# The head of the expert part of a GNN and mixture-of-experts kernel: one copy of h moved, a register load split, and other filler products on TensorE

## The chip, the cores and the metric

The kernel runs on one core of one Trainium2 chip. The metric is the device time of one execution in microseconds (us). The times of the kernel before are from three timed runs. One more execution was taken with a hardware profiler. The rows below come from that one.

## What is computed

`x` has 625 rows of 256 numbers. A graph part with 20000 edges runs first and gives x1. A feed-forward part with 8 experts follows. It sends every row to the two experts with the highest gate scores:

```python
x = x + gnn(layernorm(x), edge_index, W0, b0, W1, b1, W2, b2, Wf, bf)
xn = layernorm(x)
gate_scores = xn @ Wg + bg                          # 625 x 8
_, idx = top_k(gate_scores, 2)
mask = one_hot(idx, 8).sum(axis=-2)
h = gelu(einsum('td,edh->teh', xn, W1) + b1)        # 256 -> 512
y = einsum('teh,ehd->ted', h, W2) + b2              # 512 -> 256
out = x + einsum('ted,te->td', y, mask)
```

## The kernel before, in words

**Graph part (lines 880 to 1568).** The 20000 edges are turned into one-hot matrices on VectorE (DVE). TensorE (PE) multiplies them into a 625 x 625 count matrix. Three levels of products with that matrix follow, with each float split in a high and a low half. This part is not touched by the change.

**Routing (from L1164).** DVE adds the graph part to x, takes mean and variance, and centres the rows (`xc`). PE transposes `xc` (L1577), ScalarE (ACT) copies it out (L834), and PE makes the gate scores with 20 narrow products (L1585). DVE picks the two best experts of each row and writes the picks as 0 and 1 into `both_bf` (L1199 to L1213). PE sums them with a triangle and with ones (L1592 to L1599, the prefix sums). From these DVE works out the slot of each row: rows are sorted by expert into tiles of 128 slots, and a tile belongs to one expert. DVE then writes one-hot matrices: `hot_slot` for the first two tiles (L1262), `hot_place` and `row_in_tile` for the table of rows (L1282, L1288). The expert number of each tile stands in `owner_i` (L1253).

**The filler products.** While PE would wait in this stretch it multiplies the identity by itself into a bank that nobody reads. This is `keep_busy(n)` (L1335 to L1338). Each of its products is 128x128 float32 by 128 columns, and the profile lists it as two MATMUL records. The counts stand in L78: 12 behind the last graph product, 4 ahead of the scores, `WARM_ROUTE` = 10 between the scores and the wait for `both_bf` (L1589), and `WARM_GATHER` = 24 between the prefix sums and the wait for `hot_slot` (L1643). They are ordinary instructions of PE's queue. What stands behind them waits until they are through.

**Expert part.** `gather` (L1604) makes x of tiles 0 and 1 by products with `hot_slot`, and ACT copies it into `xt` (L862). Ten products (L1650) give `row_of`, the row behind each slot. With it GpSimd (POOL) fetches the x of later tiles by indirect DMA (L617) and adds the results into the output (L623), one scatter at a time. There are 10 fixed tiles (`FIXED`) and then a loop over pairs of tiles. In this run there are 13. A tile s goes through these steps:

- `up(s)`, PE L1620: two products of 512 columns, into `bank[1]` (tile even) or `g_ps[0]` (odd)
- `add_b1(s)`, DVE L1269: adds the expert's b1 and writes `h_pre`
- `gelu(s)`, ACT L855: `h_pre` to `h_act`
- `transpose_h(s)`, PE L1633: four transposes of `h_act` into `bank[2]`
- `h_transposed(s)`, ACT L859: copies `bank[2]` to `h_t`
- `down(s)`, PE L1639: four products into `bank[3]`
- `add_b2(s)`, DVE L1273: adds b2 and writes `y_sb`, from which POOL scatters

x of tiles from 2 on is transposed by PE (`transpose_x`, L1627) and copied by ACT (`x_transposed`, L850).

The order on each engine is written out by hand. On PE the head is up(0), up(1), transpose_h(0), down(0), transpose_x(2), transpose_h(1), up(2), transpose_x(3), down(1). On ACT it is (L863 to L869):

```python
            gelu(0, 0)
            gelu(1, 1)
            for s in range(FIXED):
                h_transposed(s)
                x_transposed(s + 2, s % 2)
                if s:
                    gelu(s + 1, (s + 1) % 2)
```

PE and DVE address the weights and biases of a tile by its expert number, which must be in a register of the engine. `first_experts` (L399 to L404) loads the numbers of the first 11 tiles with one load. PE does it at L1654, DVE at L1300, ahead of `add_b1(0)`. The load shows in the trace as TENSOR_LOAD of the engine's queue.

Of the kernel before, what the change touches and what calls it, by code (L numbers as in the profile page):

```python
# [10 lines left out]
EXPERTS = 8  # L11
# [3 lines left out]
P = 128  # L15
# [59 lines left out]

WARM_DEGREE, WARM_NORM, WARM_GATE, WARM_ROUTE, WARM_GATHER = 10, 12, 4, 10, 24  # L78


MAX_TILES = (2 * NODES + EXPERTS * (P - 1)) // P
# [3 lines left out]
FIXED = -(-2 * NODES // P)  # L85
# [4 lines left out]
def build(nc, x, src, dst, W, B, Wf, bf, Wg, bg, W1, b1, W2, b2, out):  # L90
# [8 lines left out]
    with ctx:  # L99
        def sb(name, shape, dt, scope=ctx):  # L100
            return scope.enter_context(nc.sbuf_tensor(name, shape, dt))
# [11 lines left out]
        ident = sb("ident", [P, P], f32)  # L113
        ones_sq = sb("ones_sq", [P, P], f32r)
        ones_bf = sb("ones_bf", [P, P], bf16)
# [107 lines left out]
        owner_i = sb("owner_i", [1, SLOT_TILES + 1], i32, ffn)  # L223
# [16 lines left out]
        bank = [ctx.enter_context(nc.psum_tensor(f"bank{i}", [P, 512], f32)) for i in range(2)]  # L240
# [149 lines left out]
        def gather_ps():  # L390
            return bank[0].rearrange("p (k s) -> p k s", k=KC)
# [4 lines left out]
        def odd_tile(eng):  # L396
            return eng.value_load(pairs_i[0:1, 1:2], min_val=0, max_val=1)

        def first_experts(kind):  # L399

            _, ids = nc.values_load_multi_w_load_instructions(
                owner_i[0:1, 0:FIXED + 1], engines=(kind,), min_val=0, max_val=EXPERTS - 1,
                skip_runtime_bounds_check_because="a count of at most EXPERTS, cut to EXPERTS - 1 just above")
            return ids  # L404

        def up_bank(s):
            return (bank[1], g_ps[0])[s % 2]
# [265 lines left out]
        def _(act):  # L673
# [22 lines left out]
            def chunk_starts(a):  # L696

                _, starts = nc.values_load_multi_w_load_instructions(
                    base_i[0:1, a:a + 8], engines=(mybir.EngineType.Activation,), min_val=0, max_val=NODES - 1,
                    skip_runtime_bounds_check_because="the least of a chunk's node numbers, which are below NODES")  # L700
                return starts
# [146 lines left out]
            def x_transposed(s, h):  # L848
                act.wait_ge(x_t_done, s - 1)
                act.copy(xt[:, :, h * P:(h + 1) * P], bank[0][:, 0:D].rearrange("p (k s) -> p k s", k=KC))\  # L850
                    .then_inc(xt_ready, 1)

            def gelu(s, h):
                act.wait_ge(pre_ready, s + 1)
                act.activation(h_act[:, h, :], h_pre[:, h, :], ACT.Gelu).then_inc(act_ready, 1)  # L855

            def h_transposed(s):
                act.wait_ge(t_done, s + 1)
                act.copy(h_t[:], bank[2].rearrange("p (k s) -> p k s", k=HC)).then_inc(h_t_ready, 1)  # L859

            act.wait_ge(gathered, 1)
            act.copy(xt[:], gather_ps()).then_inc(xt_ready, 2)  # L862
            gelu(0, 0)  # L863
            gelu(1, 1)
            for s in range(FIXED):
                h_transposed(s)
                x_transposed(s + 2, s % 2)
                if s:
                    gelu(s + 1, (s + 1) % 2)  # L869
            act.wait_ge(experts_ready, 2)  # L870
            more = pairs(act)
            with act.Fori(0, more) as p:
                for h in range(2):
                    s = p * 2 + (FIXED + h)
# [8 lines left out]
        def _(dve):  # L883
            n = [0]
# [382 lines left out]
            def add_b1(s, h, e):  # L1267
                dve.wait_ge(up_done, s + 1)
                dve.tensor_tensor(h_pre[:, h, :], up_bank(h)[:, :], b1_bc[:, ds(e, 1), :], ALU.add).then_inc(pre_ready, 1)  # L1269

            def add_b2(s, b, e):
                dve.wait_ge(down_done, s + 1)
                dve.tensor_tensor(y_sb[:, b, :], bank[3][:, 0:D], b2_bc[:, ds(e, 1), :], ALU.add).then_inc(y_ready, 1)  # L1273
# [23 lines left out]
            dve.scalar_tensor_tensor(row_of[:], rows_1, -1.0, unused[:], ALU.add, ALU.add).then_inc(rows_ready, 1)  # L1297
            dve.wait_ge(experts_ready, 2)
            dve.wait_ge(ffn_b_in, 16 * (EXPERTS + 1))
            e_of = first_experts(mybir.EngineType.DVE)  # L1300
            add_b1(0, 0, e_of[0])
            add_b1(1, 1, e_of[1])
            for s in range(FIXED):
                if s:
                    dve.wait_ge(act_ready, s)
                    add_b1(s + 1, (s + 1) % 2, e_of[s + 1])
                if s >= 4:
                    dve.wait_ge(scattered, 16 * (s - 3))
                add_b2(s, s % 4, e_of[s])
            more = pairs(dve)  # L1310
            with dve.Fori(0, more) as p:
                for h in range(2):
                    s = p * 2 + (FIXED + h)
# [6 lines left out]
            with dve.If(odd_tile(dve) > 0):  # L1320
                s = more * 2 + FIXED
# [5 lines left out]
        def _(pe):  # L1327
# [4 lines left out]
                pe.matmul(out_, lh, rl, start=False, stop=False, skip_group_check=True)  # L1332
                return pe.matmul(out_, ll, rh, start=False, stop=last, skip_group_check=True)  # L1333

            def keep_busy(n, free=3):  # L1335

                for _ in range(n):
                    pe.matmul(bank[free][:, 0:P], ident[:], ident[:], start=True, stop=True)  # L1338


            pe.wait_ge(consts, 4)
# [59 lines left out]
            for i, (h, c) in enumerate(Z_OUT):  # L1401
                a, b = HALVES[h]
# [166 lines left out]


            keep_busy(WARM_NORM)
            for t in range(NT):
                pe.wait_ge(xc_ready, t + 1)
                if t >= 2:
                    pe.wait_ge(xc_t_ready, t - 1)
                for k in range(KC):
                    last = pe.transpose(bank[t % 2][:, k * P:(k + 1) * P], xc[:, t, k * P:(k + 1) * P], ident[:])  # L1577
                last.then_inc(xc_t_ps, 1)
            keep_busy(WARM_GATE)
            pe.wait_ge(ffn_w_in, 16 * (2 + 2 * EXPERTS))  # L1580
            for t in range(NT):
# [4 lines left out]
                                     skip_group_check=True)  # L1586
            last.then_inc(score_ps, 1)

            keep_busy(WARM_ROUTE)  # L1589
            pe.wait_ge(both_ready, 1)  # L1590
            total, before = bank[4][:, 128:128 + EXPERTS], bank[4][:, 256:256 + NT * EXPERTS]
            pe.matmul(before, tri_bf[:], both_bf[:].rearrange("p t e -> p (t e)"), start=True, stop=False,  # L1592
                      skip_group_check=True)
            for j in range(1, NT):

                pe.matmul(before[:, j * EXPERTS:], ones_bf[:], both_bf[:, 0:NT - j, :].rearrange("p t e -> p (t e)"),
                          start=False, stop=j == NT - 1, skip_group_check=True)
# [19 lines left out]
            def up(s, h, e):  # L1617
                pe.wait_ge(xt_ready, s + 1)
                for k in range(KC):
                    last = pe.matmul(up_bank(h)[:, :], xt[:, k, h * P:(h + 1) * P], w1_sb[:, ds(e, 1), k, :],  # L1620
                                     start=k == 0, stop=k == KC - 1)
                last.then_inc(up_done, 1)
# [25 lines left out]
            for k in range(2):  # L1648
                for t in range(NT):
                    last = pe.matmul(bank[4][:, 0:SLOT_TILES], hot_place[:, k, t, :], row_in_tile[:, k, :, t],  # L1650
                                     start=k == 0 and t == 0, stop=k == 1 and t == NT - 1)
            last.then_inc(row_ps, 1)
            pe.wait_ge(experts_ready, 2)
            e_of = first_experts(mybir.EngineType.PE)  # L1654
            up(0, 0, e_of[0])
            up(1, 1, e_of[1])
            for s in range(FIXED):
# [9 lines left out]
            with pe.Fori(0, more) as p:  # L1667
                for h in range(2):
                    s = p * 2 + (FIXED + h)
# [7 lines left out]
            with pe.If(odd_tile(pe) > 0):  # L1677
                s = more * 2 + FIXED
# [27 lines left out]
```

## Time and profile before

| what | value |
|---|---|
| three timed runs, median (lowest to highest) | 203.26 us (201.93 to 204.81) |
| the profiled execution, its own time | 204.21 us |
| its span from first to last instruction | 202.4 us |
| mean granted TensorE clock in it | 0.913 of full speed |
| PE busy | 164.4 us (81%) |
| DVE busy | 100.7 us (50%) |
| ACT busy | 70.3 us (35%) |
| POOL busy | 69.8 us (34%) |

Engines work side by side, so busy times add up to more than the span. The profile names an instruction by its line in the code, and its time is counted from the start of the span. In the chain of work that ended last, PE pieces are given without overlap, each from the point where the one before it ends. In the timeline the same instructions have their full durations, which overlap.

### The profile page before, as it was taken

To read this page: it belongs to the slowest core of one execution; us is meant where nothing else is said; L and a number is where in the kernel's file an instruction comes from. 1 tells how busy PE (TensorE), PEld (TensorE's weight loads), DVE (VectorE), ACT (ScalarE), POOL (GpSimd) and SP (SyncE) were. 2 spreads that over 40 slices of the span, in tenths; PEclk is the share of its full clock that TensorE was granted. 3 is DMA by queue.
4 is the path that set the end of the run, shared out by engine and by line. 5 is a ranking of instruction groups with operands and counts; after the bars stand their busy time and mean duration, and the time that the engine had idled before them with its cause. 6 is when DMAs were issued, how large, how long until landed. Compare 5 with 4: busy or idle time off the path is not lost.

```text
span 202.4 us, 3153 instructions
## 1 busy us (share of the span) xinstructions
PE 164.4 (81%) x1013; PEld 135.6 (67%) x1014; DVE 100.7 (50%) x259; ACT 70.3 (35%) x199; POOL 69.8 (34%) x96
## 2 busy tenths in 40 slices
PE   0443575877999999999999889996999999999700
PEld 0332354766899788989899879983676677657500
DVE  7799988784660447224534876922232232223100
ACT  7234984551400136112421076013334343433200
POOL 8506910003029075002000200005555666564560
PEclk9999995585579999999999996999999999999975
DMA  5469999500000501000000179902143235432332
GB/s 144 158 165 378 367 366 368 193 0 5 3 3 0 159 5 47 7 3 3 0 3 0 48 199 279 375 32 78 11 69 80 52 52 71 77 63 26 53 52 26
DMA packets 15784, 20.34 MB, mean 100 GB/s; under 512 B 1482, under 2 KB 12116, under 8 KB 15636
## 3 DMA queue, kind: packets, MB, share of 16 engines
q1 hardware_dynamic: 12420, 15.75, 24.2%
q0 software_dynamic: 2544, 3.54, 10.5%
q10 hardware_dynamic: 800, 0.79, 1.1%
q8 instruction: 12, 0.20, 0.4%
q14 instruction: 8, 0.07, 0.1%
HBM read 16.81 MB, written 3.26 MB: 99 GB/s over the span
## 4 chain that ended last, share of the span: by engine, by line
PE 66%; DVE 13%; DMA 7%; issue 4%; ACT 4%; POOL 2%; ACTq 1%; POOLq 0%; DVEq 0%
PE cnt_ps L1639 9%; PE bank L1620 5%; PE bank L1487 5%; PE cnt_ps L1338 5%; PE g_ps L1620 4%; DMA out_rows<-y_sb,row_put 4%; PE cnt_ps L1487 4%; PE bank L1331 3%; PE g_ps L1331 3%; PE g_ps L1332 3%; PE g_ps L1333 3%; DVE hot_lo L950 2%; PE bank L1333 2%; PE bank L1332 2%; DVE a_hi L1030 2%
## 5 line engine op out<-in xcount | busy, mean ns | idle before, releaser
L1639 PE MATMUL cnt_ps<-w_sb,h_t 128*128 x104 | 24.8, 381 | 2.7 <-ACT h_t L859 2.7
L1639 PEld LDWEIGHTS cnt_ps<-w_sb,h_t 128*128 128x128 f32 x104 | 18.7, 190 | 5.2 <-issue 3.2
L623 POOL DMA_INDIRECT out_rows<-y_sb,row_of x10 | 15.9, 1586 | 15.5 <-DMA out_rows<-y_sb,row_of 11.6
L617 POOL DMA_INDIRECT xg<-x_rows,row_of x12 | 12.0, 1003 | 23.4 <-DVE row_of L1297 20.1
L1379 PE MATMUL bank<-hot_key,hot_lo 125*128 125x45 bf16 (+4 forms) x80 | 8.3, 244 | 12.8 <-DVE hot_key L953 7.9
L1379 PEld LDWEIGHTS bank<-hot_key,hot_lo 125*128 125x128 bf16 x80 | 5.3, 124 | 15.4 <-DVE hot_key L953 13.2
L1273 DVE TENSOR_TENSOR y_sb<-cnt_ps,b_bc 128x256 f32<-128x256 f32 x13 | 5.5, 425 | 20.0 <-PE cnt_ps L1639 20.0
L950 DVE TENSOR_TENSOR hot_lo<-iota_lo,edge_rel 125x1024 bf16<-125x1024 int16 x20 | 14.2, 710 | 0.9 <-PE g_ps L1379 0.7
L1338 PE MATMUL cnt_ps<-ident 128*128 128x128 f32 x100 | 13.5, 297 | 0.0
L1620 PE MATMUL bank<-w_sb,xt 128*128 x28 | 13.4, 599 | 0.1
L1338 PEld LDWEIGHTS cnt_ps<-ident 128*128 128x128 f32 x100 | 12.9, 211 | 0.0
L1620 PE MATMUL g_ps<-w_sb,xt 128*128 x24 | 11.3, 593 | 0.0
L1269 DVE TENSOR_TENSOR h_pre<-bank,b_bc 128x512 f32<-128x512 f32 x7 | 4.8, 692 | 12.5 <-PE bank L1620 12.5
L859 ACT COPY h_t<-cnt_ps 128x512 f32<-128x512 f32 x13 | 7.6, 584 | 9.6 <-PE cnt_ps L1633 9.6
L855 ACT ACTIVATE h_act<-h_pre 128x512 f32<-128x512 f32 x13 | 8.2, 629 | 7.6 <-DVE h_pre L1269 7.6
L850 ACT COPY xt<-bank 128x256 f32<-128x256 f32 x12 | 4.5, 373 | 17.6 <-PE bank L1627 17.6
L1379 PE MATMUL g_ps<-hot_key,hot_lo 125*128 125x45 bf16 (+4 forms) x80 | 8.4, 245 | 2.4 <-ACT a_hi L708 1.5
L1487 PE MATMUL bank<-a_hi,ys_hi 128*128 128x384 f32 x30 | 10.1, 337 | 0.0
L1487 PE MATMUL bank<-a_hi,ys_lo 128*128 128x384 f32 x30 | 10.1, 337 | 0.0
L953 DVE TENSOR_TENSOR hot_key<-key_tables,edge_rel 125x360 bf16<-125x360 int16 (+4 forms) x20 | 9.7, 486 | 0.0
L1331 PE MATMUL g_ps<-w_hi,ht_hi 128*128 128x256 f32 x30 | 9.6, 319 | 0.0
L1332 PE MATMUL g_ps<-w_lo,ht_hi 128*128 128x256 f32 x30 | 9.4, 313 | 0.0
(279 smaller groups left out, 433.9 us busy)
## 6 DMA issues: line engine op xcount, KB each, us to landing
w_sb<-in_L_ffn_W SPq DMA_DIRECT2D x16, 512.0 KB, 10.2
b_bc<-in_L_ffn_b SPq DMA_DIRECT2D x8, 256.0 KB, 5.3
w_stage<-in_L_gnn_W SPq DMA_DIRECT2D x3, 512.0 KB, 5.6
w_stage<-in_L_gnn_Wf SPq DMA_DIRECT2D x4, 256.0 KB, 6.4
b_bc<-in_L_ffn_b SPq DMA_DIRECT2D x1, 1024.0 KB, 12.3
x_rows<-x_f ACTq DMA_DIRECT2D x1, 640.0 KB, 8.7
x_sb<-in_x SPq DMA_DIRECT2D x1, 512.0 KB
out_rows<-x_sb SPq DMA_DIRECT2D x1, 512.0 KB
```

What stands on the lines that cost most here:

```text
L617: pool.indirect_dma_start(out=xg[:, b, :], out_offset=None, in_=x2_rows, in_offset=bass.IndirectOffsetOnAxis(ap=rows, axis=0)).then_inc(x_ ...
L623: pool.indirect_dma_start(out=out, out_offset=bass.IndirectOffsetOnAxis(ap=rows, axis=0), in_=y_sb[:, b, :], in_offset=None, compute_op=AL ...
L950: dve.tensor_tensor(hot_lo[:, u % RING:u % RING + 2, :, :], iota_lo[0:EP].unsqueeze(1).broadcast_to((EP, 2, P, CT)), rel[:, 0].unsqueeze(2 ...
L953: dve.tensor_tensor(hot_keys(u, 2), turn_keys(u // UNROLL)[0:EP].rearrange("p n w i -> p (n w) i").unsqueeze(1) .broadcast_to((EP, 2, NT * ...
L1331: pe.matmul(out_, lh, rh, start=first, stop=False, skip_group_check=True)
L1332: pe.matmul(out_, lh, rl, start=False, stop=False, skip_group_check=True)
L1333: return pe.matmul(out_, ll, rh, start=False, stop=last, skip_group_check=True)
L1338: pe.matmul(bank[free][:, 0:P], ident[:], ident[:], start=True, stop=True)
L1379: last = pe.matmul(pane(k), hot_lo[:, u % RING, :, i], hot_keys(u)[:, 0, :, i], start=i == i0, stop=i == i0 + n_i - 1, skip_group_check=True)
L1487: step = pe.matmul(z_bank(i), y[:, u, m], a_t[:, u, cols], start=first and u == 0 and y is y_parts[0], stop=last and u == NT - 1 and y is ...
L1620: last = pe.matmul(up_bank(h)[:, :], xt[:, k, h * P:(h + 1) * P], w1_sb[:, ds(e, 1), k, :], start=k == 0, stop=k == KC - 1)
L1639: last = pe.matmul(bank[3][:, 0:D], h_t[:, k, :], w2_sb[:, ds(e, 1), k, :], start=k == 0, stop=k == HC - 1)
```

## The change

Three edits, all between the gate scores and the end of tile 0.

1. ACT copies h of tile 0 (`h_transposed(0)`) between gelu(0) and gelu(1), where it stood behind gelu(1). The rest of ACT's order is as before: x_transposed(2), then for s from 1 on h_transposed(s), x_transposed(s + 2), gelu(s + 1).
2. DVE loads the expert numbers of tiles 0 and 1 first, issues add_b1(0) and add_b1(1), and then loads the other nine. PE loads its 11 with one load as before.
3. The 10 float32 filler products in the wait for `both_bf` become 36 products of `ones_bf` by `ones_bf` in bfloat16, 128x128 by 128 columns, into the same unread bank (`keep_clock`). The other three groups of fillers stay as they are.

```diff
-WARM_DEGREE, WARM_NORM, WARM_GATE, WARM_ROUTE, WARM_GATHER = 10, 12, 4, 10, 24
+WARM_DEGREE, WARM_NORM, WARM_GATE, WARM_ROUTE, WARM_GATHER = 10, 12, 4, 36, 24
...
-        def first_experts(kind):
+        def experts_of(kind, a, b):
 
             _, ids = nc.values_load_multi_w_load_instructions(
-                owner_i[0:1, 0:FIXED + 1], engines=(kind,), min_val=0, max_val=EXPERTS - 1,
+                owner_i[0:1, a:b], engines=(kind,), min_val=0, max_val=EXPERTS - 1,
...
             gelu(0, 0)
+            h_transposed(0)
             gelu(1, 1)
-            for s in range(FIXED):
+            x_transposed(2, 0)
+            for s in range(1, FIXED):
                 h_transposed(s)
                 x_transposed(s + 2, s % 2)
-                if s:
-                    gelu(s + 1, (s + 1) % 2)
+                gelu(s + 1, (s + 1) % 2)
...
-            e_of = first_experts(mybir.EngineType.DVE)
+            e_of = experts_of(mybir.EngineType.DVE, 0, 2)
             add_b1(0, 0, e_of[0])
             add_b1(1, 1, e_of[1])
+            e_of = e_of + experts_of(mybir.EngineType.DVE, 2, FIXED + 1)
...
-            def keep_busy(n, free=3):
+            def keep_busy(n):
 
                 for _ in range(n):
-                    pe.matmul(bank[free][:, 0:P], ident[:], ident[:], start=True, stop=True)
+                    pe.matmul(bank[3][:, 0:P], ident[:], ident[:], start=True, stop=True)
+
+            def keep_clock(n):
+
+                for _ in range(n):
+                    pe.matmul(bank[3][:, 0:P], ones_bf[:], ones_bf[:], start=True, stop=True)
...
-            keep_busy(WARM_ROUTE)
+            keep_clock(WARM_ROUTE)
...
-            e_of = first_experts(mybir.EngineType.PE)
+            e_of = experts_of(mybir.EngineType.PE, 0, FIXED + 1)
```

## Rows read from the trace of the kernel before

**Rows 1.** The page, chain that ended last by engine, and one costliest group (busy, mean ns | idle before)

```profile
PE 66%; DVE 13%; DMA 7%; issue 4%; ACT 4%; POOL 2%; ACTq 1%; POOLq 0%; DVEq 0%
...
L1639 PE MATMUL cnt_ps<-w_sb,h_t 128*128 x104 | 24.8, 381 | 2.7 <-ACT h_t L859 2.7
```

**Rows 2.** The chain that ended last, from the scores on: start us, us, what

```profile
121.88 3.59 PE cnt_ps L1338 x20
...
125.58 0.13 PE bank L1599 x5
125.72 5.72 PE cnt_ps L1338 x48
```

**Rows 3.** Timeline of DVE in the routing: start us, us, engine, line, operation [idle before]

```profile
124.26 0.20 DVE L1213 TENSOR_TENSOR both_bf<-both,valid 128x40 bf16<-128x40 f32 x1
125.75 0.17 DVE L1219 TENSOR_SCALAR tiles_i<-bank 128x8 int32<-128x8 f32 x1 [1.29 <-PE bank L1599]
...
129.19 1.56 DVE L1262 TENSOR_TENSOR hot_slot<-iota_p,hot_pos 128x640 fp32r<-128x640 f32 x2
```

**Rows 4.** Stretches of half a us: stretch, its length, PE busy (instructions), granted clock, DMA

```profile
122.00:122.50 0.50, 0.50 (x7) 1.00 1.13 295
122.50:123.00 0.50, 0.50 (x6) 0.72 1.15 250
123.00:123.50 0.50, 0.50 (x4) 0.50 0.65 219
...
126.00:126.50 0.50, 0.50 (x6) 0.87 1.21 373
```

**Rows 5.** Timeline of PE in the graph part: bfloat16 products, four to a row

```profile
38.81 0.56 PE L1379 MATMUL bank<-hot_key,hot_lo 125*128 125x95 bf16 x4
39.20 0.54 PE L1379 MATMUL g_ps<-hot_key,hot_lo 125*128 125x95 bf16 x4
```

**Rows 6.** A stretch of the graph part, columns as in rows 4

```profile
37.00:40.00 3.00, 2.90 (x20) 0.50 0.37 131
```

**Rows 7.** The chain that ended last, at the head of the expert part

```profile
136.63 1.73 PE g_ps L1620 x4
...
138.49 0.70 DVE h_pre L1269
...
139.22 0.63 ACT h_act L855
139.84 0.48 ACT h_t L859
...
140.46 1.97 PE cnt_ps L1639 x8
142.43 0.22 PE bank L1627 x2
142.65 0.44 PE cnt_ps L1633 x4
```

**Rows 8.** Timeline of all engines over the same stretch

```profile
137.51 0.63 ACT L855 ACTIVATE h_act<-h_pre 128x512 f32<-128x512 f32 x1 [3.04 <-DVE h_pre L1269]
...
143.12 0.58 ACT L859 COPY h_t<-cnt_ps 128x512 f32<-128x512 f32 x1
```

**Rows 9.** Register loads by line: engine, operation, duration ns min/median/max, first and last start

```profile
L401 DVEq TENSOR_LOAD <-owner_i x1: 1318/1318/1318, 135.2 to 135.2; - x1
...
L394 DVEq TENSOR_LOAD <-pairs_i x1: 313/313/313, 180.2 to 180.2; - x1
```

**Rows 10.** POOL's first gather, and the landing of the gathers of L617

```profile
136.20 1.23 POOL L617 DMA_INDIRECT xg<-x_rows,row_of  x1 [20.10 <-DVE row_of L1297]
...
DMA to landing us min/median/max: 2.7/2.8/2.9
```

**Rows 11.** The chain that ended last, from the last fixed tile to the first scatter that DMA bounds

```profile
180.16 0.44 DVE y_sb L1273
...
181.39 3.76 DMA out_rows<-y_sb,row_of
```

## The prediction

> **What bounds the kernel now.** I read the page first. The chain that ended last is two thirds PE, and the down products of the experts are its costliest group; of their 2.7 us of idle time all is put down to ACT's copy of h [rows 1]. Next I read the chain from the gate scores on, with the timelines and the granted clock beside it. Three things are to be seen.
>
> First, PE has no gap from the scores to the gather. The 20 records of the first filler group run from 121.88 for 3.59 us, the prefix sums end at 125.71, and the 48 records of the second group take 5.72 us, to 131.44, where the gather begins [rows 2]. DVE had `both_bf` ready at 124.26 + 0.20 = 124.46, and `hot_slot` at 129.19 + 1.56 = 130.75 [rows 3]. So PE comes about 1.0 us late to the first of these and 0.7 us late to the second, each time because its own fillers were not through. DVE in turn sat idle for 1.29 us before L1219 [rows 3]. The fillers are on the path.
>
> Second, the granted clock there is at its lower level (1.2 GHz) from about 122.7 to 126.1, and at 2.4 GHz on both sides: a mean of 0.72 in 122.5 to 123.0 puts the fall at 122.72, one of 0.87 puts the rise at 126.13 [rows 4]. PE was busy in all of that stretch. What it did before the fall was the narrow gate products and 0.84 us of fillers.
>
> Third, at the head of the expert part PE waits between transpose_h(0) and down(0). up(1) ends at 136.63 + 1.73 = 138.36, and down(0) starts at 140.46. Between them stand DVE's add_b1(1), ACT's gelu(1) and only then the copy of h of tile 0 [rows 7]. gelu(1) is work for tile 1, and down(0) doesn't need it.
>
> **Part 1, h of tile 0 copied ahead of gelu(1).** gelu(0) ends at 137.51 + 0.63 = 138.14 [rows 8], so PE can do transpose_h(0) as soon as up(1) is through, at 138.36. Four transposes take 0.44 us of PE, as those of tile 1 do at 142.65 [rows 7]. That gives 138.80. ACT began the copy of tile 1 at 143.12, 0.03 us behind PE's 143.09 [rows 7, 8]. So the copy of tile 0 can run from 138.83 for 0.58 us, to 139.41. It ended at 139.84 + 0.48 = 140.32 before, and down(0) followed 0.14 us later [rows 7]. Now down(0) starts at 139.55. That is **0.9 us** sooner.
>
> What is put off: h_pre of tile 1 is ready at 138.49 + 0.70 = 139.19 [rows 7], and ACT is in the copy until 139.41. gelu(1) then ends near 140.05 instead of 139.85. It is wanted by transpose_h(1), which stands on PE behind down(0) and transpose_x(2), 1.97 + 0.22 us after 139.55, at 141.74. The cover is 1.7 us. If it were gone, the 0.2 us would count in full. Next in the row is transpose_x(2) at about 141.5, which needs the first gathered tile. POOL began that gather at 136.20 and it lands 2.8 us later, at 139.0 [rows 10]. So nothing new is late. ACT's later order is unchanged, and DVE's add_b2(0) comes 0.9 us sooner with down(0).
>
> Does this reach the end? In the fixed tiles PE goes from group to group; the idle time at down outside the head is 2.7 - 1.6 = 1.1 us (1.6 us is about the gap from transpose_h(0), 138.8, to 140.46), and there is one cause for both, the copy [rows 1, 7]. At the last fixed tile the chain leaves PE through y_sb, which ends at 180.60, and 0.8 us later the scatter begins [rows 11]. From there the scatters follow one another, each behind the landing of the one before. The first of them starts from y_sb of a tile that PE sets, so it moves with PE, and the tail moves with it. I count all 0.9 us.
>
> **Part 2, the load of the expert numbers in two.** DVE's load of 11 numbers takes 1318 ns from 135.2, so it ends at 136.5. add_b1(0) waits for up(0), which ends where up(1) begins, at 136.63 [rows 7, 9]. The load is hidden by some 0.1 us, so the gain is 0 and at most 0.1. `row_of` and up(0) both hang on the same PE products, so the cover stays when both move. One number alone takes 313 ns; that makes (1318 - 313) / 10 = 100 ns for each further one, so the nine cost an estimated 1.1 us. They are issued behind add_b1(1), from about 138.5, and are through at 139.7, or at 140.3 if they wait for its end at 139.19. Behind the load on DVE's queue stands add_b2(0), wanted at 139.55 + 1.97 = 141.5. The cover is at least 1.2 us. **I take 0.**
>
> **Part 3, 36 bfloat16 products for 10 float32 ones.** No row shows a bfloat16 product of 128 adjacent columns. The nearest is the filler itself. Of the second group 0.41 us lie ahead of 126.13; the 46 records behind it take 5.31 us, 0.115 us each. Of the first group 7 records fill 0.84 us, and 13 take the other 2.75 us at the lower clock, 0.21 us each [rows 2, 4]. A record is half a float32 product. I take a bfloat16 product at half a record: 0.058 and 0.106 us. From above it is bounded by the products of the graph part, with 95 columns and strided operands: 0.39 / 4 = 98 ns at the lower clock [rows 5, 6], which makes 132 ns for 128 columns, and 66 ns at the upper. From below it is bounded by 128 columns at one column a cycle, 0.053 us and 0.107 us, which is my value within the reading.
>
> With the clock falling at 122.72 as before, 15 products go by in 0.84 us and the other 21 take 2.2 us: PE is through at 125.0, not 125.47 (at 125.8 by the upper bound). The prefix sums move by 0.45 us. But the second group then starts that much sooner inside the stretch at the lower clock, where it does half the work. From 125.27 to 126.13 it does 4 records, the other 44 take 5.06 us, and it ends at 131.2 against 131.44. `hot_slot` comes at 130.3 and is still ahead. So **0.2 us** is gained; the bounds are 0.2 lost and 0.3 gained.
>
> The float32 records show no time for loading the stationary operand: 0.21 us at 1.2 GHz is 254 cycles, and two passes of 128 columns are 256. The last five prefix products, with a load each, take 0.13 us, 26 ns each [rows 2]. The Trainium skill ("TensorE: Matmul & The Clock Gate", section "The mechanism" of Part 3) has a rule that speaks against me: a load overlaps a running matmul only where the two use different row groups of the array, and the fillers use all rows (the same section also lets a load into the second weight buffer go ahead). By that each of the 36 would pay up to 26 ns more, and the group would end near 125.7, later than now. The float32 rows don't show it, and I keep 0.2 us; the bound above covers it.
>
> **The sum.** 0.9 + 0 + 0.2 = 1.1 us, for the profiled execution from 204.21 to 203.1 us. That execution lies 0.95 us above the median of the timed runs. Nothing says that another execution will do so, so I take the 1.1 us off the median: 203.26 - 1.1 = **202.2 us**, 0.5% less. About 2% (4.1 us) is what a measurement of this kernel can tell from no change, so the forecast counts as no change.
>
> **The rivals.**
>
> *The clock stays up.* If the lower clock doesn't come between 122.7 and 126.1, the 36 products end at 121.88 + 36 x 0.058 = 124.0 and PE waits for `both_bf` at 124.46. The prefix sums end near 124.7 instead of 125.71. The 48 records then take 5.5 us to 130.2, and `hot_slot` is there at 129.75. The gather starts 1.2 us sooner, with part 1 it is 2.1 us: 201.2 us. For it: PE was at 2.4 GHz when the new products would begin. Against it: 0.84 us of dense fillers stood before the fall in the kernel before too, and the narrow products ahead of them are unchanged [rows 4]. The Trainium skill (same page, section "What's actually happening") says that the moments at which the clock may change are not tied to the start of a kernel. By that, the low stretch would lie elsewhere in other executions, before and after the change alike, and the worth of part 3 would vary from run to run. The one trace here can't show it. Of this rival's price only part is a difference between kernels: an execution before, with the clock up, also has it.
>
> *The bfloat16 products hold the clock less well, and the time goes up.* In the graph part, where PE's work is bfloat16 products of up to 95 columns mixed with float32 ones [rows 5], the clock was at the lower level at 37 to 40 us with PE busy for 2.90 of 3.00 us [rows 6]. If the new fillers count for less than the old ones, the lower clock lasts beyond 126.1. As long again would be to 129.5. Then the second group does 20 records by then and 28 at 0.115 us behind it, and ends at 132.75: 1.3 us late, less the 0.9 us of part 1, 0.4 us slower, 203.7 us. It decides once the lower clock outlasts 126.13 by some 2 us, as each us there costs half a us. Against it: from 125.3 on the unchanged float32 fillers run, and they stood ahead of the rise before.
>
> *The copy moves and the end doesn't.* If down(0) starts sooner but transpose_x(2) then waits for its gather, or the scatters set the pace from tile 0 on, part 1 is given back: 203.0 us. Against it are the 2.5 us between landing and use, and scatters that start 0.8 us after y_sb even at the last fixed tile [rows 10, 11]. For it: the last scatters are bound by one another, and 3.76 us of landing with 0.8 us of issue make 4.6 us, against 1.73 + 1.97 + 0.22 + 0.44 = 4.4 us of PE for a tile [rows 7, 11].
>
> **How the numbers follow.** I give the forecast 0.62, the clock that stays up 0.18, the slower case 0.10, the lost copy 0.10. The timed runs differ from their median by 1.3 and 1.5 us, which blurs all four. The range runs from 200.8, a little below the second case, to 203.8, just past the slower one. Beyond 2%, below 199.2 or above 207.3, nothing of this leads; 0.03 and 0.02 remain for what I don't see, 0.95 for within 2%.
>
> **What would show it.** Right for part 1: ACT has the copy of L859 ahead of the second gelu, down(0) starts 0.9 us sooner counted from the end of up(1), and PE's gap there falls from 1.6 to 0.7 us. Right for part 2: add_b1(0) stays about 0.15 us behind the end of up(0), with a short TENSOR_LOAD ahead of it and a longer one behind add_b1(1), and add_b2(0) waits for PE alone. Right for part 3: 36 bfloat16 records of 0.06 to 0.11 us, the prefix sums 0.4 us sooner counted from the scores, and the gather 0.2 us. Wrong: a low clock beyond 126.1 or none at all, a second group that begins at `both_bf` without delay, a wait of transpose_x(2) for a DMA, or scatters further apart than PE's tiles from the start.

## The result and the profile after

| | before | after |
|---|---|---|
| median (lowest to highest), 20 executions each | 203.66 us (201.93 to 205.23) | 202.11 us (200.47 to 202.98) |
| profiled execution, its own time | 204.21 us | 202.68 us |
| its span | 202.4 us | 200.8 us |
| mean granted TensorE clock in it | 0.913 | 0.925 |

The ratio after to before is 0.9925, with a 95% interval of 0.9902 to 0.9948. That is 1.5 us less (1.1 to 2.0). It is less than 2%, and still clear of no change. I predicted 202.2 us, from 200.8 to 203.8. Here and below a ratio leaves out the executions that are more than 1.5% above the fastest of their kernel, while medians and counts are of all executions.

The page of the kernel after, busy time by engine, and the granted clock in 40 slices of the span:

```profile
PE 162.8 (81%) x1029; PEld 133.9 (67%) x1030; DVE 100.7 (50%) x259; ACT 70.4 (35%) x199; POOL 69.8 (35%) x96
...
PEclk9999995585579999999999999999999999999985
```

The same line of the kernel before:

```profile
PEclk9999995585579999999999996999999999999975
```

The 6 behind the middle is the low stretch of [rows 4]. It is gone after. The chain that ended last, from the scores to tile 1 (start us, us, what):

```profile
120.10 2.15 PE bank L1592 x20
...
124.61 0.21 DVE both_bf L1214
124.82 0.05 issue
124.86 0.19 PE bank L1599
...
125.27 5.46 PE cnt_ps L1340 x48
130.73 0.12 PE bank L1618
130.85 0.12 PE bank L1620
...
135.92 1.72 PE g_ps L1627 x4
137.64 0.51 PE cnt_ps L1640 x4
...
138.17 0.59 ACT h_t L859
138.77 0.13 issue
138.90 1.97 PE cnt_ps L1646 x8
140.87 0.22 PE bank L1634 x2
141.09 0.44 PE cnt_ps L1640 x4
```

Three readings. Between the end of the scores (122.25) and the prefix sums the chain now runs through DVE and `both_bf`, where it ran through PE's own fillers [rows 2]. From the end of the scores to the gather it is 130.73 - 122.25 = 8.48 us, and was 131.44 - 121.88 = 9.56: 1.08 us less. From the end of up(1) to down(0) it is 138.90 - 137.64 = 1.26 us, and was 2.10 [rows 7]: 0.84 us less. DVE and ACT's gelu have left the chain there. The scores themselves came 0.37 us later in this execution. 1.08 + 0.84 - 0.37 = 1.55 us, and the spans differ by 1.6.

The granted clock behind the scores, and the new fillers (columns as in rows 4 and rows 3):

```profile
122.50:123.00 0.50, 0.50 (x13) 1.00 0.97 315
```

```profile
122.09 2.17 PE L1345 MATMUL cnt_ps<-ones_bf 128*128 128x128 bf16 x36
124.86 0.19 PE L1599 MATMUL bank<-both_bf,tri_bf 128*128 128x40 bf16 x1 [0.61 <-DVE both_bf L1214]
```

All 36 products run at the upper clock. A row of 219 ns each that ends 2.17 us after it begins leaves (2.17 - 0.22) / 35 = 56 ns from one start to the next. I took 58. PE then waits 0.61 us for `both_bf`. ACT around tile 0:

```profile
136.80 0.63 ACT L855 ACTIVATE h_act<-h_pre 128x512 f32<-128x512 f32 x1 [3.03 <-DVE h_pre L1270]
138.17 0.59 ACT L859 COPY h_t<-cnt_ps 128x512 f32<-128x512 f32 x1 [0.75 <-PE cnt_ps L1640]
138.66 0.63 ACT L855 ACTIVATE h_act<-h_pre 128x512 f32<-128x512 f32 x1
```

The second gelu stands behind the copy and ends at 139.29. Its reader, transpose_h(1), starts at 141.09, so the cover is there.

### The profile page after: what moved, and what is told of

Same layout as the page of the kernel before. It is cut to its first block, busy times and chain, and to the rows that moved or that the text cites. A ratio compares the mean times of both kernels' runs of the same rounds, so it can differ in the third digit from the quotient of the medians.

```text
span 200.8 us, 3186 instructions
## 1 busy us (share of the span) xinstructions
PE 162.8 (81%) x1029; PEld 133.9 (67%) x1030; DVE 100.7 (50%) x259; ACT 70.4 (35%) x199; POOL 69.8 (35%) x96
## 4 chain that ended last, share of the span: by engine, by line
PE 66%; DVE 14%; DMA 7%; issue 4%; ACT 3%; POOL 2%; ACTq 1%; POOLq 0%; DVEq 0%
PE cnt_ps L1646 9%; PE bank L1627 5%; PE bank L1494 5%; PE g_ps L1627 4%; DMA out_rows<-y_sb,row_put 4%; PE cnt_ps L1494 4%; PE cnt_ps L1340 3%; PE bank L1333 3%; PE g_ps L1333 3%; PE g_ps L1335 3%; PE g_ps L1334 3%; DVE hot_lo L951 2%; PE bank L1335 2%; PE bank L1334 2%; PE cnt_ps L1640 2%
## 5 line engine op out<-in xcount | busy, mean ns | idle before, releaser
L617 POOL DMA_INDIRECT xg<-x_rows,row_of x12 | 12.0, 1004 | 22.4 <-DMA x_rows<-x_f 19.0
L1340 PE MATMUL cnt_ps<-ident 128*128 128x128 f32 x80 | 9.5, 276 | 0.0
L1335 PE MATMUL g_ps<-w_hi,ht_lo 128*128 128x256 f32 x30 | 9.4, 314 | 0.0
```

Of the source, the lines that this page charges most:

```text
L617: pool.indirect_dma_start(out=xg[:, b, :], out_offset=None, in_=x2_rows, in_offset=bass.IndirectOffsetOnAxis(ap=rows, axis=0)).then_inc(x_ ...
L1340: pe.matmul(bank[3][:, 0:P], ident[:], ident[:], start=True, stop=True)
```

## The experiments

All of them start from the kernel before or the changed kernel, with one edit. "Ratio" is to the kernel before, measured beside it on the same chip. From each trace I read three numbers: whether the lower clock came behind the scores, the time from the end of the scores to the gather, and the time from the end of up(1) to down(0). The last two are read from the chain, which counts a PE instruction only from the end of the one before. The first product of the gather starts some 0.24 us before the last filler ends. "From idle" means that PE waited for `hot_slot` before the gather, so that its first product counts from its own start. Such a number compares with the others when 0.24 is added.

| run | median us (executions) | ratio (95%) | lower clock behind the scores | scores to gather | up(1) to down(0) |
|---|---|---|---|---|---|
| before | 203.66 (20) | 1 | from 122.72, 0.84 behind them | 9.56 | 2.10 |
| before_again | 204.38 (12) | 1.0023 (0.9988 to 1.0058) | 0.57 behind | 9.56 | 2.10 |
| before_look | 202.32 (1) | | 0.19 behind | 9.66 | 2.10 |
| load_only | 203.81 (12) | 1.0016 (0.9982 to 1.0050) | none | 8.49 | 2.10 |
| h_only | 202.99 (12) | 0.9947 (0.9914 to 0.9980) | none | 8.48 | 1.33 |
| bf16_only | 203.02 (12) | 0.9962 (0.9923 to 1.0000) | none | 8.49 | 2.10 |
| after | 202.11 (20) | 0.9925 (0.9902 to 0.9948) | none | 8.48 | 1.26 |
| after_look | 202.94 (1) | | none | 8.48 | 1.27 |
| nine_f32 | 202.99 (12) | 0.9947 (0.9919 to 0.9976) | 0.79 behind | 9.34 | 1.26 |
| ones_f32 | 202.35 (12) | 0.9949 (0.9912 to 0.9985) | 0.14 ahead of their end | 9.43 | 1.27 |
| six_f32 | 203.54 (12) | 0.9958 (0.9915 to 1.0000) | 0.31 ahead | 8.61 | 1.27 |
| route0 | 203.82 (10) | 1.0010 (0.9975 to 1.0045) | 2.8 behind | 10.07 | 1.26 |
| gather22 | 202.17 (12) | 0.9902 (0.9866 to 0.9938) | none | 8.20, from idle | 1.26 |
| all_bf | 202.31 (12) | 0.9915 (0.9873 to 0.9957) | with their end | 9.06, from idle | 1.27 |

before_again is the kernel before itself, and its median is 0.6 us above that of the executions beside it (203.80). A difference of that size between two medians is noise, and one of 0.8 is not far above it.

**The three parts, each alone.** h_only:

```diff
             gelu(0, 0)
+            h_transposed(0)
             gelu(1, 1)
-            for s in range(FIXED):
+            x_transposed(2, 0)
+            for s in range(1, FIXED):
                 h_transposed(s)
                 x_transposed(s + 2, s % 2)
-                if s:
-                    gelu(s + 1, (s + 1) % 2)
+                gelu(s + 1, (s + 1) % 2)
```

> Part 1 alone. The copy theory (down(0) hung on the copy behind gelu(1), nothing else is late next) expects 0.8 to 0.9 us less than the kernel before, and a gap of 1.2 to 1.3 us from the end of up(1) to down(0), where it was 2.1. The rival (the copy moves, a gather or the scatters then set the pace) expects the same short gap and less than 0.3 us at the end.

The median is 0.8 us under that of the kernel before beside it (203.80), and the ratio says 1.1 (0.4 to 1.8). The interval is clear of the rival's 0.3, and the gap is short as expected. The copy theory holds. Its chain has the same short way as the changed kernel's:

```profile
136.16 1.72 PE g_ps L1621 x4
137.88 0.58 PE cnt_ps L1634 x4
...
138.48 0.59 ACT h_t L859
...
139.21 1.97 PE cnt_ps L1640 x8
```

bf16_only:

```diff
-WARM_DEGREE, WARM_NORM, WARM_GATE, WARM_ROUTE, WARM_GATHER = 10, 12, 4, 10, 24
+WARM_DEGREE, WARM_NORM, WARM_GATE, WARM_ROUTE, WARM_GATHER = 10, 12, 4, 36, 24
...
-            keep_busy(WARM_ROUTE)
+            keep_clock(WARM_ROUTE)
```

> Part 3 alone. The kind theory (bfloat16 products of ones keep the clock at its upper level where float32 ones did not) expects 0.7 to 1.1 us less than before and no stretch at the lower clock between the scores and the gather. The chance theory (the lower clock comes or doesn't, whatever the fillers; only PE's lateness changes) expects 0.2 to 0.6 us less, and the low stretch in as many executions as before.

0.8 us less, from 0 to 1.6. The sizes of both theories lie in that interval, so the time alone doesn't decide. The trace has no low stretch.

load_only:

```diff
-            e_of = first_experts(mybir.EngineType.DVE)
+            e_of = experts_of(mybir.EngineType.DVE, 0, 2)
             add_b1(0, 0, e_of[0])
             add_b1(1, 1, e_of[1])
+            e_of = e_of + experts_of(mybir.EngineType.DVE, 2, FIXED + 1)
```

> Part 2 alone. The cover theory (the load of 11 numbers ended 0.1 us before up(0) did) expects no change, ratio 0.998 to 1.002, and add_b1(0) 0.15 us behind the end of up(0) as before. The rival (the load was part of the path) expects 0.1 us or more less and a shorter gap there. As its fillers are float32, its trace also shows once more whether the lower clock comes behind the scores: kind theory, it does or not by the execution, and its executions spread in mean clock like those of the kernel before, down to 0.913.

No change: 203.81 beside 203.83. The cover theory holds. add_b1(0) started at 136.13, and up(0) ended where up(1) begins on the chain, at 135.98: 0.15 us, as before.

In order: the chain, the timeline of DVE, and the loads by line.

```profile
135.98 1.73 PE g_ps L1621 x4
```

```profile
136.13 0.69 DVE L1269 TENSOR_TENSOR h_pre<-bank,b_bc 128x512 f32<-128x512 f32 x1 [1.48 <-PE bank L1621]
```

```profile
L401 DVEq TENSOR_LOAD <-owner_i x2: 540/1304/2069, 134.6 to 137.9; - x2
```

The second load took 2069 ns where I had estimated 1.1 us of work, or 1.8 us from its start if it waits for add_b1(1). It began at 137.9, while add_b1(1) ran from 137.84 to 138.53, so such a wait can be some 0.7 us of it; no run shows whether it is. It still ended at 140.0, ahead of add_b2(0) at 141.92. The trace has a second use. Its fillers are float32, no lower clock came behind the scores, and the gather starts at 8.49 us, like the changed kernel's. Float32 fillers are not late when the clock is up, since PE waits for `both_bf` behind them:

```profile
124.92 0.19 PE L1593 MATMUL bank<-both_bf,tri_bf 128*128 128x40 bf16 x1 [0.30 <-DVE both_bf L1213]
```

The parts add up: 0.8 + 0.8 + 0.0 = 1.6 us by the medians, against 1.5 for the change. By the ratios it is 1.1 + 0.8 - 0.3, which is 1.6 too, but each of the three is known to some 0.7 us only.

**Kind or chance.** nine_f32 is the changed kernel with float32 fillers of the same PE time:

```diff
-WARM_DEGREE, WARM_NORM, WARM_GATE, WARM_ROUTE, WARM_GATHER = 10, 12, 4, 36, 24
+WARM_DEGREE, WARM_NORM, WARM_GATE, WARM_ROUTE, WARM_GATHER = 10, 12, 4, 9, 24
...
-            keep_clock(WARM_ROUTE)
+            keep_busy(WARM_ROUTE)
```

> The changed kernel with 9 float32 fillers (the PE time of 36 bfloat16 ones) in the wait for both_bf. Kind theory: the low stretch is back, the gather starts some 1.0 us later counted from the scores, the time is 0.5 to 0.9 us above the changed kernel's, so only about 0.9 us under the kernel before. Chance theory: within 0.2 us of the changed kernel, 1.3 to 1.7 us under the kernel before.

Its median lies 0.9 us above the changed kernel's and exactly at h_only's. The ratios are only 0.5 us apart, with overlapping intervals, so the pair alone doesn't show by its times that part 3 is gone. All the kernels with part 1 together say more. The three with bfloat16 in this group (after, and gather22 and all_bf with a further edit each) have ratios of 0.9902 to 0.9925, the four with float32 (h_only, nine_f32, ones_f32, six_f32) 0.9947 to 0.9958, and the means of the two lie 0.7 us apart. In the trace of nine_f32 the low stretch is back, and the gather starts 0.86 us later:

```profile
122.25 3.21 PE cnt_ps L1340 x18
125.46 0.03 PE bank L1599
...
125.72 5.88 PE cnt_ps L1340 x48
```

The kernel before once more:

> The kernel before once more, for its granted clock in each execution. Ratio 1.000 within the interval. Kind theory: the low stretch between 122 and 127 us is in its trace again. Chance theory: it may be there or not, and the mean clock of its executions spreads like that of the changed kernel.

The low stretch is there again, with 9.56 us to the gather. What these runs give beyond their own trace is the mean clock of each execution. The lowest values, 0.904 to 0.915, are those of executions with a low stretch behind the scores, where traces exist for them (before 0.913, before_again 0.912, nine_f32 0.915). An execution can also have that stretch at a higher mean, as before_look at 0.936 and all_bf at 0.955, so they are not all of them. The kernel before ran in three sets beside the others, and there they come in 9 of 35, 6 of 35 and 3 of 23 executions. They come in 5 of 12 of before_again, 4 of 12 of load_only, 2 of 12 of h_only and 3 of 12 of nine_f32. That makes 32 of 141 with 9 or 10 float32 identity products, or 23%. In the four kernels with bfloat16 fillers (after, bf16_only, gather22, all_bf) they come in 0 of 56, and the lowest value is 0.921. But 12 of these 56, or 21%, lie at 0.924 to 0.927, where after and after_look lie, whose traces are like that of the kernel before without the low stretch behind the scores. So it looks as if the same share of executions had only lost that stretch; for executions without a trace this is not shown.

The traces can be paired as well. The clock is low in the graph part too, and where it is low differs between executions. Five executions have the same history there, with two low stretches at the same times within 0.4 us. The second low stretch in them, and the routing (stretch, PE busy, granted clock, DMA), first before_again:

```profile
44.00:58.00 14.00, 12.39 (x58) 0.52 0.02 4
...
120.00:127.00 7.00, 7.00 (x58) 0.76 0.93 275
```

and nine_f32:

```profile
44.00:58.00 14.00, 12.39 (x58) 0.52 0.01 4
...
120.00:127.00 7.00, 7.00 (x59) 0.76 1.03 275
```

and after:

```profile
44.00:58.00 14.00, 12.39 (x58) 0.51 0.02 4
...
120.00:127.00 7.00, 6.39 (x84) 1.00 0.96 276
```

The other two are the kernel before, which is like before_again, and after_look, which is like after. Two more executions share another history, first before_look:

```profile
44.00:58.00 14.00, 12.39 (x75) 0.76 0.02 4
...
120.00:127.00 7.00, 7.00 (x57) 0.76 1.01 327
```

and gather22, whose fillers behind the scores are the bfloat16 ones:

```profile
44.00:58.00 14.00, 12.39 (x75) 0.76 0.02 4
...
120.00:127.00 7.00, 6.39 (x83) 1.00 1.01 332
```

So with the same history up to the scores, four executions with float32 fillers fall and three with bfloat16 fillers don't. PE was busy for all of 7.00 us where the clock fell, and for 6.39 us where it stayed. The two float32 executions that don't fall, load_only and h_only, share neither history: they have one more low stretch, at 72 to 76 us.

One more trace of each of the two kernels:

> A further trace of the kernel before. By the reading so far the gather starts 9.4 to 9.6 us behind the end of the scores where the lower clock comes behind them, and 8.5 us where it doesn't, with float32 fillers too. No third value.

> A further trace of the changed kernel. No stretch at the lower clock between the scores and the gather, and 8.5 us from the end of the scores to the gather. If the stretch is there after all, the bfloat16 fillers only make it rarer.

Both as expected by the first part of each: 9.66 us with the low stretch, 8.48 without. 9.66 is a little above the range that I gave, since nearly the whole first group ran at the lower clock (3.96 us for 20 records):

```profile
120.17 3.96 PE cnt_ps L1338 x20
124.14 0.02 PE bank L1592
```

**Type or values.** The new fillers differ from the old ones in type and in values: dense ones for an identity. ones_f32 has 9 float32 products of ones.

```diff
-WARM_DEGREE, WARM_NORM, WARM_GATE, WARM_ROUTE, WARM_GATHER = 10, 12, 4, 36, 24
+WARM_DEGREE, WARM_NORM, WARM_GATE, WARM_ROUTE, WARM_GATHER = 10, 12, 4, 9, 24
...
-                    pe.matmul(bank[3][:, 0:P], ones_bf[:], ones_bf[:], start=True, stop=True)
+                    pe.matmul(bank[3][:, 0:P], ones_sq[:].bitcast(f32), ones_sq[:].bitcast(f32), start=True, stop=True)
```

> The changed kernel with 9 float32 products of ones by ones in the wait for both_bf: the type of the old fillers with the values of the new ones. If what holds the clock is the type, it is like nine_f32: about 203.0 us, executions with a mean clock near 0.915 among it. If it is the values (dense ones for a mostly empty identity), it is like the changed kernel: about 202.1 us, its lowest class of mean clock near 0.925.

Inconclusive. The median, 202.35, lies between the two, and the ratio, 0.9949, is that of nine_f32. Mean clocks of 0.914 and 0.915 come in 2 of 12 executions, which no bfloat16 kernel had, and this speaks for the type. The trace can't help: the clock fell at 120.28, before the first filler.

```profile
120.00:120.50 0.50, 0.50 (x5) 0.78 0.75 252
120.50:121.00 0.50, 0.50 (x3) 0.50 1.88 266
```

The scores ended at 120.42, and a mean of 0.78 puts the fall at 120.28.

**How many fillers.** six_f32 is nine_f32 with 6, route0 the changed kernel with none:

> The changed kernel with 6 float32 fillers in the wait for both_bf, so that PE is through ahead of both_bf at either clock. If the gain of part 3 is PE's lateness alone, it equals the changed kernel within 0.2 us. If the clock has a price of its own (the second filler group is slowed where the low stretch reaches into it), it is 0.3 to 0.6 us above the changed kernel and 0.2 to 0.5 us under nine_f32; the class of executions with a mean clock near 0.915 is there again.

> The changed kernel without fillers between the scores and both_bf, so that PE idles 2.6 us there. Kind theory: fillers are needed to hold the clock; the lower clock comes behind the scores and the second group is slowed, 0.4 to 1.3 us above the changed kernel. Rival (fillers there do nothing but make PE late): equal to the changed kernel.

six_f32: in its trace the gather starts 8.61 us behind the scores in spite of the low stretch, 0.73 us less than in nine_f32. So a low stretch that ends early costs little when no filler stands in the way. Its low stretch came 1.1 us sooner than that of nine_f32, so not all of the 0.73 is the count. Its median over all 12 executions is 0.55 us above nine_f32, outside what I expected. Four of them, at mean clocks of 0.904 to 0.912, have spans of 202.9 to 203.3 us, and the ratio doesn't count them. The median of the other eight is 202.63 us, 0.5 above the changed kernel and 0.4 under nine_f32, as expected. So the trace foretold the eight and not the four, and six fillers are not shown to be better or worse than nine.

route0: PE was idle for 2.6 us, the clock fell at 124.26, and the second group ran 7.04 us instead of 5.46:

```profile
124.37 0.13 PE bank L1606 x5
124.50 7.04 PE cnt_ps L1340 x48
```

That is 1.6 us in the trace (10.07 us to the gather) and 1.7 us by the medians, more than I expected. The bfloat16 fillers there are worth about as much as the whole change (1.5 us), and without them all of it is gone.

**Is PE still late to hot_slot?** gather22 has 22 float32 fillers ahead of the gather instead of 24:

> The changed kernel with 22 float32 fillers ahead of the gather, not 24. In the changed kernel's trace the group ended at 130.73 and hot_slot at 130.29, so the theory that PE is still 0.44 us late there expects 0.4 us less than the changed kernel (201.7 us beside its 202.1). The rival (the gather then waits on something else, or the clock falls with fewer fillers) expects no gain or a loss.

The theory fails in the trace. hot_slot is ready at 128.39, and now PE waits for it:

```profile
126.87 1.52 DVE hot_slot L1263 x2
128.40 0.14 issue
128.53 0.36 PE bank L1618
128.89 0.11 PE bank L1620
```

The idle PE starts 0.14 us behind hot_slot. Its first product then takes 0.36 us. It takes as long in the changed kernel, by the timeline, where it overlaps the last fillers:

```profile
130.49 0.36 PE L1618 MATMUL bank<-hot_slot,x_hi 128*128 128x256 f32 x1
```

That start is 0.20 us behind hot_slot (130.29), not 0.44: the 130.73 of the chain is where the last filler ended, and the gather had begun by then. Counted from the scores, the end of the first product comes at 128.89 - 120.33 = 8.56 us, and in the changed kernel at 130.85 - 122.25 = 8.60. So 0.04 us is gained, not 0.4. The median, 202.17, equals the changed kernel's. The ratio, 0.9902, is a little lower, with the intervals well inside one another, so a gain of a few tenths is neither shown nor excluded.

all_bf has bfloat16 in all four groups and 88 for the 24 ahead of the gather:

```diff
-WARM_DEGREE, WARM_NORM, WARM_GATE, WARM_ROUTE, WARM_GATHER = 10, 12, 4, 36, 24
+WARM_DEGREE, WARM_NORM, WARM_GATE, WARM_ROUTE, WARM_GATHER = 10, 48, 16, 36, 88
...
-            keep_busy(WARM_GATHER)
+            keep_clock(WARM_GATHER)
```

> The changed kernel with all four filler groups of the routing in bfloat16 at the same PE time, the last one shortened from 24 float32 to 88 bfloat16 products (5.1 us). If bfloat16 fillers hold the clock and PE was 0.4 us late to hot_slot, it is 0.3 to 0.6 us under the changed kernel, 201.6 us or less, and the gather starts 8.1 us behind the end of the scores. Rival: no gain over the changed kernel, as the other groups weren't at a lower clock.

No gain shown: 202.31 us, with a ratio of 0.9915 whose interval holds the changed kernel's 0.9925. And its trace shows where bfloat16 fillers stop helping:

```profile
118.87 2.19 PE bank L1592 x20
121.06 3.65 PE cnt_ps L1345 x36
```

The clock fell at 121.04, as the narrow products of the scores ended, so no filler behind them could prevent it, and the 36 products took 3.65 us instead of 2.0 (36 times 56 ns). The 16 bfloat16 fillers ahead of the scores didn't prevent it either. The 8.1 us that I expected with the clock up stays untested. No version was shown to beat the changed kernel.

## Why the prediction was right, and where it wasn't

**The number.** 202.2 against 202.11. That it is so close is luck, since two errors cancel in it. I predicted 1.1 us less and 1.5 came. And I took it off the median of three executions, 203.26, where 20 give 203.66.

**Part 1, 0.9 us: right.** 0.84 in the trace (2.10 to 1.26), 0.77 in h_only, 0.8 at the end by its median. The copy started 0.02 us behind the transposes as I had it. The transposes took 0.51 to 0.58 us on the chain, and not 0.44, which is what is missing from 0.9. transpose_x(2), the scatters and the tail moved with it: y_sb of the last fixed tile and its scatter are still 1.2 us apart, start to start [rows 11], so nothing was given back.

```profile
178.60 0.44 DVE y_sb L1274
...
179.83 3.74 DMA out_rows<-y_sb,row_of
```

**Part 2, 0 us: right,** by load_only. The second load took 2070 ns, against an estimated 1.1 us of work, or 1.8 with a wait for add_b1(1), and the cover that I gave as 1.2 us or more was 1.1 us in the trace after, from 137.8 + 2.07 = 139.9 to add_b2(0) at 141.0.

**Part 3, 0.2 us: the size was wrong.** It measured 0.8 by bf16_only (0 to 1.6), 0.9 by the medians and 0.5 by the ratios as the changed kernel against nine_f32, and 1.08 in the profiled pair. The times alone would leave room for 0.2; the traces don't. The step that failed was the first one of its sum, "With the clock falling at 122.72 as before". I took the fall as given, with the fillers only changing the work inside it. The rival "the clock stays up" is what happened in the profiled pair: the gather 1.2 us sooner was its price, and 1.08 came. The median, 202.11, stays 0.9 us above its 201.2. What I held against it, that 0.84 us of dense fillers stood ahead of the fall before, was true and no argument, since those were float32 products of the identity. What I also held, that an execution of the kernel before can have the clock up, is shown: load_only and h_only have it and get to the gather in 8.49 and 8.48 us without any change of theirs there. So by the traces part 3 buys about 1.1 us in the executions where the clock would have fallen and nothing in the others. Its 0.8 fits the six traces with 9 or 10 float32 identity products, four of which have the low stretch: 4/6 of 1.1 is 0.7.

**The first-order reading of PE's lateness** was right in its place and wrong in its cause. PE was 1.0 us late to `both_bf` because its fillers ran at the lower clock. With the clock up, in load_only, the same 10 products are through 0.2 us ahead of it (124.62 against 124.86). The 0.7 us of lateness at the gather was 0.3: the gather's first product began at 131.19, 0.44 us behind `hot_slot`, and 0.14 of that an idle PE needs too, as gather22 shows. The chain counts PE without overlap, and so made it look later than it was.

**The slower rival,** bfloat16 products that hold the clock less well, is the opposite of what the runs show. Its argument was a stretch of the graph part in which PE also did float32 work and waited, and it carried little. **The lost copy** is excluded by h_only.

**The rule that I weighed.** The trace after has 56 ns from start to start, with a weight load for each of the 36 products, and I had taken 53 ns for 128 columns alone. So a load of the whole array costs an estimated 3 ns at most here, not 26. The Trainium skill's sentence that a load overlaps a running product only in other row groups ("TensorE: Matmul & The Clock Gate", "The mechanism" of Part 3) doesn't hold for these; its lines on the second weight buffer do. The same page (section "Wait — 56ns, not 53.3ns?") gives 55.6 ns for such products at the upper clock, and the trace agrees. My sum for the rule was also wrong: 36 times 26 ns behind 125.0 is 125.9, not 125.7, and the bound of 125.8 didn't cover it.

**Left open.** Why bfloat16 fillers hold the clock where float32 ones don't: the type, the number of instructions, or the values. ones_f32 leans to the type and doesn't settle it. A kernel with bfloat16 identity products was not tried.

## What to carry to other kernels

A filler product is chosen by what it does to the granted clock. Before costing an edit of fillers, ask what happens if the clock doesn't fall, price it as its own case, and look at the mean clock of many executions and not at one trace. And where an engine seems a few tenths late behind fillers, compare the start of its next instruction in the timeline, not the end of the last filler, with the time at which the data was there, and subtract what an idle engine needs to start. In a serial head of a pipeline, put first on each engine what the next group of the bound engine waits for: every trace with that edit has the gap shorter by 0.77 to 0.84 us.

## What the runs showed that I had not expected

- With 9 or 10 float32 identity fillers behind the narrow products the clock fell in four of six traces, and with 36 bfloat16 ones in one of five (all_bf, where it fell before they began). Executions at a mean clock of up to 0.915 went from 32 of 141 to 0 of 56.
- A register load on DVE's queue of 9 numbers took 2070 ns, one of 2 numbers 540 ns, where one of all 11 took 1318 ns. The time doesn't follow from the count. The load of 9 began while DVE was still adding for tile 1, 0.7 us before the end of that; whether it waited for it wasn't tried.
- An idle PE started 0.14 us behind the DVE instruction it waited for. The first product of the gather took 0.36 us from its start in both cases, idle or not; behind fillers 0.24 us of it overlap them, and the chain doesn't count these.
- Without fillers between the scores and `both_bf`, PE was idle for 2.6 us, the clock fell at the end of that, and the time was 1.7 us longer.
